# Two moves between engines in a graph network kernel: one comparison of the counting loop from ScalarE to VectorE, and the second edge layer's drop rows turned in place of its messages

## The reference, cut to what matters

```python
def _L1_gnn_ref(h, Wm1, bm1, Wm2, bm2, Wu1, bu1, Wu2, bu2, drop_mask, src, dst):
    e = jnp.concatenate([h[src], h[dst]], axis=-1)
    e = jax.nn.relu(e @ Wm1 + bm1) @ Wm2 + bm2
    e = e * drop_mask
    m = jax.ops.segment_sum(e, dst, num_segments=n)
    z = jnp.concatenate([h, m], axis=-1)
    h_new = jax.nn.relu(z @ Wu1 + bu1) @ Wu2 + bu2
    return h_new
...
    h = jnp.maximum(_layernorm(x, axis=-1), 0.0)
    x = x + _L1_gnn_ref(h, ..., edge_attr_96, src, dst)
```

## Time and profile before

| | us |
|---|---|
| median of 3 runs (6116.01 to 6123.38) | 6119.12 |
| the profiled execution's own time | 6117.6 |
| its span, first to last instruction | 6115.7 |
| counting, 52 to 494 us of the span | 442 |
| second edge layer, 2500 to 3390 us of the span | 890 |

### The profile page before, as it was taken

One profiled execution on the slowest core, in us unless ns is written; L12 is line 12 of the kernel. 1 busy time (PEld: TensorE's weight loads), 2 busy tenths in 40 slices (PEclk: granted clock), 3 DMA queues, 4 the chain that ended last, 5 costly groups with the idle time before them and its releaser, 6 DMA issues. The chain is left out here.

```text
span 6115.7 us, 115642 instructions
## 1 busy us (share of the span) xinstructions
PE 4559.9 (75%) x22351; PEld 2931.6 (48%) x22351; DVE 4229.4 (69%) x13899; ACT 3505.4 (57%) x8824; POOL 3410.0 (56%) x3543
## 2 busy tenths in 40 slices
PE   5776888888799999799999788878888984222222
PEld 1223555555444444466666566656656663222221
DVE  5667888888788888777777688878876663222222
ACT  6996666666699999555555455545545552111110
POOL 0004666666654443344343566566657776777777
PEclk9999999999999999899999787778778885555555
DMA  0002333333344443455555577656657773222222
GB/s 18 0 0 67 101 105 102 104 103 105 98 96 94 94 94 86 105 143 142 141 142 137 150 188 193 181 148 163 163 144 183 184 187 89 61 64 66 63 67 57
DMA packets 1144861, 677.32 MB, mean 111 GB/s; under 512 B 898421, under 2 KB 1096833, under 8 KB 1144744
## 3 DMA queue, kind: packets, MB, share of 16 engines
q1 hardware_dynamic: 1031784, 527.07, 31.7%
q0 software_dynamic: 112960, 148.99, 11.7%
HBM read 445.59 MB, written 232.61 MB: 111 GB/s over the span
## 5 line engine op out<-in xcount | busy, mean ns | idle before, releaser
L724 POOL DMA_INDIRECT xs<-t,idx x1176 | 1110.5, 944 | 951.5 <-DMA idx<-at 573.4
L1197 PE MATMUL bank<-ident,msg 128*96 128x128 f32 (+1 forms) x1568 | 305.5, 329 | 856.5 <-ACT msg L992 771.8
L724 POOL DMA_INDIRECT xs<-c,idx x784 | 763.9, 974 | 291.6 <-issue 233.2
L992 ACT ACTIVATE msg<-xs,now 128x96 f32<-128x96 f32 x784 | 229.3, 364 | 1071.4 <-DMA xs<-c,idx 715.3
L1041 PE MATMUL bank<-cols,before 128*128 128x384 f32 x1756 | 734.0, 520 | 17.3 <-DVE wu_out L1334 14.1
L1495 DVE TENSOR_TENSOR_SCAN aggT<-goes,aggT,bank 96x512 f32<-96x512 f16 (+1 forms) x490 | 620.7, 1267 | 133.9 <-PE bank L1150 115.0
L1197 PEld LDWEIGHTS bank<-ident,msg 128*96 128x96 f32 (+1 forms) x1568 | 218.6, 163 | 1022.7 <-ACT msg L992 650.1
L1208 PE MATMUL bank<-w,aggT 96*128 96x96 f32 (+1 forms) x3136 | 549.9, 334 | 105.2 <-DVE aggT L1495 104.6
L1670 DVE SCALAR_TENSOR_TENSOR y<-bank,now,rows 128x96 f32<-128x96 f32 x392 | 97.2, 310 | 719.1 <-PE bank L1208 719.1
L724 POOL DMA_INDIRECT xd<-in_x_dram,idx x392 | 373.9, 954 | 395.5 <-DVE xn L1565 228.6
L1208 PEld LDWEIGHTS bank<-w,aggT 96*128 96x128 f32 (+1 forms) x3136 | 517.3, 249 | 130.9 <-issue 88.6
(11 more groups left out here) (233 smaller groups left out, 10943.2 us busy)
## 6 DMA issues: line engine op xcount, KB each, us to landing
t<-xn SPq DMA_DIRECT2D x294, 192.0 KB, 2.2
xd<-t SPq DMA_DIRECT2D x294, 192.0 KB, 3.5
goes<-goes_d SPq DMA_DIRECT2D x392, 128.0 KB
xd<-in_x_dram SPq DMA_DIRECT2D x196, 192.0 KB
t<-xo SPq DMA_DIRECT2D x196, 192.0 KB
hd<-t SPq DMA_DIRECT2D x196, 192.0 KB
hs<-t SPq DMA_DIRECT2D x196, 192.0 KB
c<-xn SPq DMA_DIRECT2D x196, 192.0 KB
```

Source lines behind the costliest of these rows:

```text
L724: nc.gpsimd.indirect_dma_start(out=into, out_offset=None, in_=table, in_offset=bass.IndirectOffsetOnAxis(ap=indices, axis=0)).then_inc(don ...
L1197: ins = nc.tensor.transpose(bank[g.at(2)][0:m, c * P:(c + 1) * P], msg[:, g.at(2), c, 0:m], ident[:])
```

## The change

In counting, DVE makes the destination's high part with one more comparison (128 columns, f16) and gives three signals a round in place of two; ACT makes the source's alone: one square and one relu over 128 columns.

In the second edge layer the messages are made transposed, as one product into bank 2. The drop rows are brought to the same layout: `turn_drop` transposes them on PE into bank 5, with lag 1, behind `home_u` and ahead of `tr`; the new `drop_copy` on ACT copies them from bank 5 to tanh_g, with lag 2, between `hidden` and `home_act`. `times_drop` multiplies bank 2 with tanh_g into msgT (512 columns on 96 partitions in place of 384 on 128), and `sums` scans msgT. `turn_messages` goes. The drop rows' slot is free once they are turned.

```diff
--- before.py
+++ after.py
@@ -366,7 +366,7 @@
         more("attr", (EG - 1) % 3, 16)
         e0["root"] = Count(sem("root_e0"))
         e1 = Phase(EG, dict(mx=1, norm_s=1, norm=1, tr_s=1, tr=1, evac_s=1, evac=1, hid=1, act=1, tok=1, msg=1, seg=1,
-                            agg=1, z=1, g=1, u=1, xr=1, zh=1, gh=1, uh=1, fin_h=1), dict(edge_slots, h_out=(3, 1, 1), x_in=(6, 1, 1), res=(6, 1, 1)))
+                            gate=1, agg=1, z=1, g=1, u=1, xr=1, zh=1, gh=1, uh=1, fin_h=1), dict(edge_slots, h_out=(3, 1, 1), x_in=(6, 1, 1), res=(6, 1, 1)))
         more("attr", (EG - 1) % 3, 16)
         e1["root"] = Count(sem("root_e1"))
         nd = Phase(NG, dict(my=1, norm=1, t1=1, r1=1, z1=1, g1=1, u1=1, x1=1),
@@ -564,7 +564,7 @@
                     if ph is e0:
                         need(sp, ph["tr_s"], g.j - 2)
                     else:
-                        need(sp, ph["msg"], g.j - 2)
+                        need(sp, ph["seg"], g.j - 2)
                     sp.sem_inc(sp_turn, 1)
                     first = g.j * GE
                     if is_last_group(g, EG):
@@ -829,12 +829,10 @@
 
             def hot_rows(g):
                 need(act, counted, g.j - 1)
-                for which in range(2):
-                    ins = nc.scalar.activation(apart[:, g.at(2), which, :], iota_hi[:], ACT.Square,
-                                               bias=hi_of[:, which, bass.ds(g.j, 1)], scale=-1.0)
-                ins.then_inc(hot_his, 1)
+                nc.scalar.activation(apart[:, g.at(2), 0, :], iota_hi[:], ACT.Square,
+                                     bias=hi_of[:, 0, bass.ds(g.j, 1)], scale=-1.0).then_inc(hot_his, 1)
                 need(act, hot_his, 2 * g.j + 1)
-                nc.scalar.activation(hot_hi[:, g.at(2), :, :], apart[:, g.at(2), :, :], ACT.Relu, bias=1.0, scale=-1.0)\
+                nc.scalar.activation(hot_hi[:, g.at(2), 0, :], apart[:, g.at(2), 0, :], ACT.Relu, bias=1.0, scale=-1.0)\
                     .then_inc(hot_his, 1)
 
             act.wait_ge(col_step, 8)
@@ -942,6 +940,11 @@
                     nc.scalar.activation(m1[0:D, g.at(2), :], bank[2][0:D, :], ACT.Relu, bias=bias[:, 3:4])\
                         .then_inc(ph["act"].sem, 1)
 
+                def drop_copy(g):
+                    need(act, ph["seg"], g.j + 1)
+                    need(act, ph["msg"], g.j - 1)
+                    nc.scalar.activation(tanh_g[:, g.at(2), :], bank[5][0:D, :], ACT.Copy).then_inc(ph["gate"].sem, 1)
+
                 def home_act(g):
                     need(act, ph["zh"], g.j + 1)
                     need(act, ph["uh"], g.j - 1)
@@ -967,7 +970,7 @@
                     pipelined(act, EG, [(evac_d, 1), (update_act, 3), (hidden, 1), (edge_y, 4), (half_gate, 1),
                                         (norms, 0), (evac_s, 0)])
                 else:
-                    pipelined(act, EG, [(update_act, 4), (hidden, 2), (home_act, 1), (norms, 0), (evac_s, 0)])
+                    pipelined(act, EG, [(update_act, 4), (hidden, 2), (drop_copy, 2), (home_act, 1), (norms, 0), (evac_s, 0)])
 
             for k, ph in enumerate(conv):
                 def rows_in(g):
@@ -1015,7 +1018,7 @@
 
 
             def count(g):
-                need(pe, hot, 2 * (g.j + 1))
+                need(pe, hot, 3 * (g.j + 1))
                 need(pe, hot_his, 2 * (g.j + 1))
                 for which in range(2):
                     for side in range(2):
@@ -1138,16 +1141,13 @@
                         products(bank[4][0:D, :], mw2[:], m1[:, g.at(2), :], ph["tok"])
                         return
                     need(pe, ph["act"], g.j + 1)
+                    products(bank[2][0:D, :], wm2[:], m1[:, g.at(2), :], ph["tok"])
+
+                def turn_drop(g):
+                    need(pe, ph["attr"][g.at(3)], attr_landed(g))
+                    need(pe, ph["gate"], g.j)
                     for c in range(G):
-                        ins = nc.tensor.matmul(tok(bank[2])[:, c, :], m1[:, g.at(2), c * P:(c + 1) * P], wm2[:],
-                                               start=True, stop=True)
-                    ins.then_inc(ph["tok"].sem, 1)
-
-                def turn_messages(g):
-                    need(pe, ph["msg"], g.j + 1)
-                    need(pe, ph["agg"], g.j)
-                    for c in range(G):
-                        ins = nc.tensor.transpose(bank[5][0:D, c * P:(c + 1) * P], msg[:, g.at(2), c, 0:D], ident[:])
+                        ins = nc.tensor.transpose(bank[5][0:D, c * P:(c + 1) * P], drop[:, g.at(3), c, :], ident[:])
                     ins.then_inc(ph["seg"].sem, 1)
 
                 def upd_z(g):
@@ -1182,8 +1182,8 @@
                 if first:
                     pipelined(pe, EG, [(hid, 1), (upd_u, 3), (messages, 1), (upd_z, 2), (tr, 0)])
                 else:
-                    pipelined(pe, EG, [(upd_z, 4), (hid, 2), (turn_messages, 3), (home_z, 1), (upd_u, 4), (messages, 2),
-                                       (home_u, 1), (tr, 0)])
+                    pipelined(pe, EG, [(upd_z, 4), (hid, 2), (home_z, 1), (upd_u, 4), (messages, 2),
+                                       (home_u, 1), (turn_drop, 1), (tr, 0)])
                     need(pe, ph["fin_h"], EG)
                 need(pe, ph["xr"], EG)
 
@@ -1278,6 +1278,8 @@
                 for which in range(2):
                     nc.vector.tensor_scalar(hot_lo[:, g.at(2), which, :], iota_lo[:],
                                             lo_of[:, which, bass.ds(g.j, 1)], None, ALU.is_equal).then_inc(hot, 1)
+                nc.vector.tensor_scalar(hot_hi[:, g.at(2), 1, :], iota_hi[:], hi_of[:, 1, bass.ds(g.j, 1)], None,
+                                        ALU.is_equal).then_inc(hot, 1)
 
             pipelined(dve, ET, [(one_hot, 0)])
 
@@ -1542,11 +1544,11 @@
 
                 def times_drop(g):
                     need(dve, ph["tok"], g.j + 1)
-                    need(dve, ph["attr"][g.at(3)], attr_landed(g))
+                    need(dve, ph["gate"], g.j + 1)
                     dve.sem_inc(dve_turn, 1)
-                    need(dve, ph["seg"], g.j - 1)
-                    nc.vector.tensor_tensor(msg[:, g.at(2), :, 0:D], tok(bank[2]),
-                                            drop[:, g.at(3), :, :], ALU.mult).then_inc(ph["msg"].sem, 1)
+                    need(dve, ph["agg"], g.j - 1)
+                    nc.vector.tensor_tensor(msgT[:, g.at(2), :], bank[2][0:D, :], tanh_g[:, g.at(2), :], ALU.mult)\
+                        .then_inc(ph["msg"].sem, 1)
 
                 def new_y(g):
                     need(dve, ph["u"], g.j + 1)
@@ -1606,7 +1608,7 @@
                     stages = [(new_y, 4), (edge_moments, 0), (moments_y, 4), (times_g(ph), 5), (times_gate, 2), (new_x, 5),
                               (sums, 2), (with_b, 0), (of_round, 0, EG + 4)]
                 else:
-                    sums = sums_of(ph, lambda g: bank[5][0:D, :], ph["seg"], D, ph["z"])
+                    sums = sums_of(ph, lambda g: msgT[:, g.at(2), :], ph["msg"], D, ph["z"])
                     stages = [(spread, 2), (times_drop, 3), (home_x, 2), (new_x, 5), (edge_moments, 0), (of_round, 0), (sums, 3)]
                 pipelined(dve, EG, stages)
                 need(dve, ph["z"], EG)
```

## The result

The changed kernel takes 6074.2 us (median of 4 runs, 6066.2 to 6079.3), the kernel before 6120.7 beside it: ratio 0.9925, 95% interval 0.9909 to 0.9941, about 46 us less. The forecast was 6079 us.

A forecast was written before the change was run, and what follows sets the result against it. No engine is full: rings of waits through PE and ScalarE bound counting and the second edge layer. 6117.6 - 16 (counting) - 23 (edge layer) = 6078.6, say 6079 us; own range 6064 to 6093, 8 in 10 within 6056 to 6108.

The forecast's parts named there:

- the ring through VectorE: Counting, PE to VectorE and back over two buffers: 2.16 us for two rounds, the new bound, 16 us less.
- the one through ScalarE: Counting, PE to ScalarE and back: 2.24 us for two rounds before, at most 1.92 after the change.
- the 0.04 for the late start once in a turn of the loop: Counting: every six rounds VectorE starts 0.36 after PE instead of 0.25, adding 0.04 us over the three pairs.
- The first rival: Counting: third comparison adds 0.23 or more, or PE starts later after DVE; no counting gain, 6095 us; chance 0.22.
- The second rival: Edge layer: ACT's copy without overlap or waiting for signals, g 1.26 after m1, 6098 us; chance 0.08.
- the scan's idle time: Edge layer, VectorE: 1.04 us idle before sums, to go once it reads msgT and not PE's bank.
- PE's own sum: Edge layer: PE's work in a round stays at 8.3 us and is not the bound.
- the ring through ScalarE: Edge layer, from PE's turn of hd through m1, g and norms: 9.02 to 8.78 us a round, 23 us less.
- the load's room: Edge layer: drop rows' load is issued some 10 us before their turn; loads of equal size land in 3.4 us.

The follow-up runs named there:

- the doubled one: Changed kernel with VectorE's new counting comparison made twice, the second into a spare tile, PE waiting for it: 6098.6 us (0.9976).
- the turn in the old place: Changed kernel with turn_drop between hid and home_z, lag 2 instead of 1: 6095.3 us (0.9964).
- one exchange in PE's list: Kernel before the change with home_z moved ahead of turn_messages on PE, nothing else: 6076.0 us (0.9930).
- the fastest kernel: Changed kernel plus three counting buffers, drop_copy after evac_s, upd_z behind home_z, upd_u before tr, update_act last, new_x and edge store a step later: 5916.0 us (0.9672).

## Why the prediction was right

- **Counting's bound.** Foretold: the ring through VectorE takes the place of the one through ScalarE, 2.16 for two rounds, 16 us less. It did, at 2.13 and 21 us. The terms: the comparison takes 0.248 us (0.23 foretold) and starts 0.09 before the one ahead of it ends, so it adds 0.16 to 0.17 (0.15 foretold); PE starts 0.13 after VectorE (0.14 foretold). The term that was wrong is the 0.04 for the late start once in a turn of the loop: after the change VectorE starts 0.25 after PE in every round.
- **The overlap.** The new comparison starts at 422.36, while the one before it runs until 422.45, and the doubled one cost 0.16 of its 0.25. The first rival, which rested on the whole duration, fell with it. The Trainium skill (VectorE: DVE Perf Modes, The DRAIN you can't avoid) says that the next operation does not start until the pipe of the one before is empty, and adds that one which is not held starts earlier; the start 0.09 before the recorded end agrees with the addition. So does that page's section on two instructions with no wait between them, by which only a held instruction waits until all earlier ones have finished.
- **The edge layer.** Foretold: a round of 8.78 by a copy of 0.578 that overlaps 0.10 with what stands beside it, 23 us. Measured: 8.77, 0.581, m1 ending at 2912.64 with the copy started at 2912.54, and 25.9 us, 23.5 of them from 94 rounds; most of the rest is one round while the pipeline fills, 10.7 us before and 8.8 after, for a reason that no run here shows. The second rival (no overlap) is excluded by that line, and the turn in the old place shows that the ring is the right one.
- **What should hide, hid.** The multiplication takes 0.69 (0.68 foretold) and the scan's idle time is gone. PE's own sum, foretold to stay at 8.3, is 8.77 - 0.54 = 8.23, which changes nothing while the ring through ScalarE sets the round. PE shows no wait for a transfer ahead of the drop rows' turn; loads of that size land in 3.5 us. That the load's room is 10 us was not tried by making it later.
- **The sum.** 6079 against 6074.2: counting gave 5 us and the edge layer 3 us more than forecast. Against that, the execution from which the sum starts (6117.6) lay 3 us under the median of the kernel before that was run beside the change (6120.7), so a part of the closeness is chance.

## What to carry to other kernels

Find the ring before the engine: write down the chain from one buffer's release to its next release, with the idle time at each step, and ask of every instruction whether it stands on that chain; four transposes, 0.43 us together, cost all of it in one place of a list and nothing in another, as long as the ring sets the round. Before a new data layout is built, try the order alone: one exchange in PE's list was worth nearly the whole change. And where a ring spans few buffers, a third buffer may be worth more than moving work between engines, and it decides what such a move is worth (84 us against 21).

## What I had not expected of the hardware

With three buffers, three VectorE operations of 0.44, 0.44 and 0.27 us (means of that run) go through in 0.83 us a round for hundreds of rounds, over a quarter less than the sum of their durations and with no gap for the waits between rounds. PE's turn of hd takes 0.48 when PE had to wait for it and 0.44 when it had not. In the fastest kernel PE did the edge layer's round in 8.20 us, at a granted clock of 1.00 (its 2.4 GHz level) from 2550 to 3100 us, as in the kernel before; in that stretch it was busy for 550.00 of 550 us, and for 515.49 before.
